# The stretch ahead of the loop of a fused attention and feed-forward kernel: who rounds and squares the second weight matrix, and in which order the queues are written

## The reference

```python
x = x + conv_ref(ln_over_channels(x))      # attention
t = tokens(x)                              # 16 x 192 tokens of 512 channels
t = t + ffn_ref(ln(t), w1, w2)

def conv_ref(x):
    avg, mx = mean(x over pixels), max(x over pixels)
    x = x * sigmoid(mlp(avg) + mlp(mx))            # fc1, relu, fc2
    s = concat(mean(x over channels), max(x over channels))
    return x * sigmoid(conv7x7(s))

def bitlinear(x, w):
    rms = rsqrt(max(mean(w * w), EPS))
    wq = clip(round(w * rms), -1, 1) / rms          # weights of -1, 0, 1
    scale = 127 / max(max|x| of each token, EPS)
    return (round(x * scale) / scale) @ wq.T

def ffn_ref(x, w1, w2):                             # 512 -> 2048 -> 512
    return bitlinear(gelu(bitlinear(x, w1)), w2)
```

## Time and profile before

| | us |
|---|---|
| median of 3 runs | 311.19 |
| lowest, highest | 310.03, 312.21 |
| the profiled execution | 311.29 |
| its span in the trace | 309.3 |
| TensorE busy | 265.9 |
| VectorE busy | 249.7 |
| ScalarE busy | 217.1 |
| GpSimd busy | 165.6 |

### The profile page before, as it was taken

How to read it: one execution, slowest core, us unless ns; L and a number is a source line. 1 busy time by engine, 2 the same in 40 slices (tenths; PEclk the granted TensorE clock), 3 DMA queues, 4 the chain that set the end, 5 groups by cost and what they waited for, 6 DMA issues and landing times.

```text
span 309.3 us, 5830 instructions
## 1 busy us (share of the span) xinstructions
PE 265.9 (86%) x1826; PEld 153.4 (50%) x1834; DVE 249.7 (81%) x556; ACT 217.1 (70%) x442; POOL 165.6 (54%) x267
## 2 busy tenths in 40 slices
PE   2457659696699999999999999999999987999974
PEld 2345634564356465645565555555555544444431
DVE  0673889989699989998998999899989997788410
ACT  1863687579476978687778876787678846676831
POOL 9506655416855385648555765566656563346410
PEclk9999965969999999999999999999999999899998
DMA  7999100002253129412931393439223713073693
GB/s 202 389 392 401 45 1 0 2 2 57 42 141 70 24 46 246 96 34 54 252 72 35 69 237 70 37 69 256 53 50 72 151 39 68 17 174 72 74 209 102
DMA packets 71077, 34.19 MB, mean 111 GB/s; under 512 B 52040, under 2 KB 68424, under 8 KB 70536
## 3 DMA queue, kind: packets, MB, share of 16 engines
q1 hardware_dynamic: 69300, 32.78, 43.1%
q10 hardware_dynamic: 1748, 1.05, 1.2%
HBM read 14.94 MB, written 6.29 MB: 69 GB/s over the span
## 4 chain that ended last, share of the span: by engine, by line
DVE 40%; PE 36%; issue 10%; ACT 4%; POOL 4%; ACTq 2%; DMA 1%; another core or an unknown queue 1%; SPq 1%; DVEq 0%; POOLq 0%
PE ps_o L1201 12%; DVE amax L883 8%; PE ps_h L1190 6%; PE ps_t L1190 6%; DVE t L856 6%; PE front L1120 3%; DVE st L858 3%; DVE amax L869 3%; DVE pv L824 3%; PE small L1166 2%; DVE cen L868 2%; DVE junk_v L909 2%; DVE st L782 2%; PE front L1210 2%; DVE res L900 2%
## 5 line engine op out<-in xcount | busy, mean ns | idle before, releaser
L1201 PE MATMUL ps_o<-w2T,hq 128*128 128x512 f16 x384 | 92.7, 379 | 1.1 <-DMA hq<-w_raw 1.1
L488 POOL TENSOR_SCALAR w_room<-w_room,q 128x1024 f32<-128x1024 f32 x48 | 57.1, 1201 | 51.4 <-DVE q L893 50.9
L883 DVE TENSOR_REDUCE amax<-w_room 128x1 f32<-128x1024 f32 (+1 forms) x48 | 57.2, 1208 | 2.3 <-ACT w_room L550 2.2
L1190 PE MATMUL ps_h<-w1T,xq 128*128 128x512 f16 x208 | 54.0, 403 | 1.1 <-ACT xq L550 0.7
L1201 PEld LDWEIGHTS ps_o<-w2T,hq 128*128 128x128 f16 x384 | 36.3, 98 | 36.0 <-DMA hq<-w_raw 2.1
L550 ACT ACTIVATE w_raw<-w_room 128x1024 f16<-128x1024 f16 x48 | 50.4, 1052 | 0.6 <-POOL w_room L488 0.6
L550 ACT ACTIVATE w_room<-ps_h,s 128x512 f32<-128x512 f32 x52 | 35.0, 688 | 13.1 <-PE ps_h L1190 12.0
L1190 PE MATMUL ps_t<-w1T,xq 128*128 128x512 f16 x176 | 42.0, 382 | 0.0
L550 ACT ACTIVATE w_room<-ps_t,s 128x512 f32<-128x512 f32 x44 | 30.2, 687 | 8.0 <-PE ps_t L1190 5.6
L1190 PEld LDWEIGHTS ps_h<-w1T,xq 128*128 128x128 f16 x208 | 20.1, 103 | 23.9 <-issue 3.9
L550 ACT ACTIVATE junk_m<-front 128x192 bf16<-128x192 f32 x64 | 20.6, 332 | 14.7 <-DVE pooled L795 14.7
(11 more groups left out here) (125 smaller groups left out, 450.5 us busy)
## 6 DMA issues: line engine op xcount, KB each, us to landing
out<-w_room SPq DMA_DIRECT2D x16, 384.0 KB, 3.0
x_in<-in_x SPq DMA_DIRECT2D x14, 384.0 KB, 5.1
w_room<-in_L_ffn_w SPq DMA_DIRECT2D x4, 1024.0 KB, 8.8
w_raw<-in_L_ffn_w SPq DMA_DIRECT2D x4, 1024.0 KB, 12.0
x_in<-in_x ACTq DMA_DIRECT2D x2, 384.0 KB, 3.8
hq<-w_raw SPq DMA_TRANSPOSE x48, 3.1
fc_raw<-in_L_conv_fc_w ACTq DMA_DIRECT2D x2, 128.0 KB, 4.2
taps_rev<-in_L_conv_sa_w SPq DMA_DIRECT2D x1, 0.2 KB
```

The lines of the kernel that those rows point to most:

```text
L488: pool.tensor_scalar(part, part, q2[tile.par][:, 0:1], MAGIC, ALU.mult, ALU.add).then_inc(g_rounded, 1)
L883: chain.mark(dve.tensor_reduce(amax2[:, i:i + 1], w1_room[:, first + i * F // 2:first + (i + 1) * F // 2 + i], AX.X, ALU.max, apply_absolu ...
L1190: last = pe.matmul(banks[b], xq[tile.pair.par][:, tile.s, k, :], w1T[:, k, b * 512:(b + 1) * 512], start=(k == 0), stop=(k == NC - 1))
L1201: last = pe.matmul(ps_o[:, :], hq[tile.par][:, k, :], w2T[:, k, :], start=(k == 0), stop=(k == NF - 1))
```

## The change

All edits are ahead of the loop. The loop's bodies are the same.

- SyncE issues five of the eight tap loads, ScalarE three.
- ScalarE squares three quarters of w2 instead of two, VectorE one instead of two. ScalarE does the first two earlier: one ahead of pair 0's channel gate, one ahead of pair 0's channel sums. The third comes behind the first gelu of tile 0.
- GpSimd rounds all of w2, in eight pieces, behind `round_x` of tile 1. VectorE rounds none.
- GpSimd normalises pair 1 in two steps around `round_x` of tile 0, and pair 2 in two steps around `round_g` of tile 1.
- On TensorE the convolution of pair 0 stands ahead of the second turn of w1 instead of the third; tile 0's four blocks alternate with pair 1's four turns; tile 1's blocks and pair 1's gates alternate with w2's eight turns; two of pair 2's three turns of x stand ahead of w2's last turns. ScalarE's and VectorE's lists follow that.

```diff
-        SQUARES_BY_VECTOR = [(3,), (2, 3)]
+        SQUARES_BY_VECTOR = [(3,), (3,)]
...
-            load_taps(sp, range(W // 2))
+            load_taps(sp, range(W - 3))
...
             def round_weights(k, raw):
                 pool.wait_ge(w_rms_ready, k + 1)
-                for i in range(4) if k == 0 else (1, 3):
+                for i in range(4):
                     part = quarter(k, raw, i)
-                    pieces = (part[:, 0:2, :], part[:, 2:4, :]) if k == 0 else (part,)
+                    pieces = (part[:, 0:2, :], part[:, 2:4, :]) if k == 0 else (part[:, 0:F // 2], part[:, F // 2:F])
...
             round_weights(0, w1_raw)
-            normalise1(Pair(1), 0, 1, 2)
             rstd2(Tile(Pair(0), 0))
+            normalise1(Pair(1), 0, 1)
             round_x(Tile(Pair(0), 0))
+            normalise1(Pair(1), 2)
             weight_rms(1)
-            round_weights(1, w2_raw)
             rstd2(Tile(Pair(0), 1))
             round_x(Tile(Pair(0), 1))
+            round_weights(1, w2_raw)
             round_g(Tile(Pair(0), 0))
             rstd2(Tile(Pair(0), 2))
             round_x(Tile(Pair(0), 2))
+            normalise1(Pair(2), 0, 1)
             round_g(Tile(Pair(0), 1))
-            normalise1(Pair(2), 0, 1, 2)
+            normalise1(Pair(2), 2)
...
-            load_taps(act, range(W // 2, W))
+            load_taps(act, range(W - 3, W))
...
             squares(0, w1_raw, w1_loaded, (2,))
+            squares(1, w2_raw, w2_loaded, (0,))
             gate_channels(pair0)
             copy_caT(pair0)
+            squares(1, w2_raw, w2_loaded, (1,))
             for s in range(NT):
                 sum_channels(Tile(pair0, s))
...
-            copy_weights(0, (0, 2))
+            copy_weights(0, (0,))
             gate_tokens(pair0)
-            copy_weights(0, (4, 5, 6, 7))
-            squares(1, w2_raw, w2_loaded, (0,))
+            copy_weights(0, (2, 4, 5, 6, 7))
...
             def weight_sum(k):
-                dve.wait_ge(squares_done, 3 + 2 * k)
+                dve.wait_ge(squares_done, 3 + 3 * k)
...
-            def round_weights(k, raw):
-
-                dve.wait_ge(w_rms_ready, k + 1)
-                for i in (0, 2):
-                    part = quarter(k, raw, i)
-                    dve.tensor_scalar(part, part, w_rms[:, k:k + 1], MAGIC, ALU.mult, ALU.add).then_inc(w_even_rounded, 1)
...
             def turn_weights(k, raw, banks):
                 for n in banks:
-                    i = n // 2
-                    if k == 0:
-                        pe.wait_ge(w_pool_rounded, n + 1)
-                    elif i % 2:
-                        pe.wait_ge(w_pool_rounded, 8 + i // 2 + 1)
-                    else:
-                        pe.wait_ge(w_even_rounded, i // 2 + 1)
+                    pe.wait_ge(w_pool_rounded, 8 * k + n + 1)
...
-            turn_weights(0, w1_raw, (0, 1))
+            turn_weights(0, w1_raw, (0,))
             pe.wait_ge(band_ready, 2)
             conv(pair0)
-            turn_weights(0, w1_raw, (2, 3, 4, 5, 6, 7))
+            turn_weights(0, w1_raw, range(1, 8))
```

More of the change, by code:

```diff
@@ L662, in _ @@
             act.wait_ge(masks_ready, 2)
[L663 removed]
+            copy_weights(0, (0,))
             gate_tokens(pair0)
[L665 to L666 removed]
+            copy_weights(0, (2, 4, 5, 6, 7))
             copy_xq(Tile(pair0, 0), 0)
+            gelu(Tile(pair0, 0), None, h_start, (0,))
+            squares(1, w2_raw, w2_loaded, (2,))
             token_mean(pair1, 0, 1)
[L669 to L673 removed]
+            gelu(Tile(pair0, 0), None, h_start, (1,))
+            token_mean(pair1, 1, 0)
+            gelu(Tile(pair0, 0), None, h_start, (2,))
+            token_mean(pair1, 2, 1)
+            gelu(Tile(pair0, 0), None, h_start, (3,))
+            token_mean(pair1, 3, 0)
+            copy_xq(Tile(pair0, 1), 1)
+            gelu(Tile(pair0, 1), None, h_start, (0,))
             copy_weights(1, (0,))
[L675 to L676 removed]
             gate_channels(pair1)
+            gelu(Tile(pair0, 1), None, h_start, (1,))
+            copy_caT(pair1)
+            copy_weights(1, (2,))
+            gelu(Tile(pair0, 1), None, h_start, (2,))
+            sum_channels(Tile(pair1, 0))
+            copy_weights(1, (3,))
+            sum_channels(Tile(pair1, 1))
+            gelu(Tile(pair0, 1), None, h_start, (3,))
+            sum_channels(Tile(pair1, 2))
             copy_weights(1, (4,))
[L679 to L680 removed]
+            copy_x(Tile(pair2, 0), 1)
+            copy_x(Tile(pair2, 1), 0)
             copy_weights(1, (6, 7))
[L682 to L687 removed]
             pack_g(Tile(pair0, 0), 0)
             pack_g(Tile(pair0, 0), 1)
[L690 to L692 removed]
+            copy_xq(Tile(pair0, 2), 1)
             copy_x(Tile(pair2, 2), 0)
@@ L901, in add_ffn, with squares @@
                                          t[tile.pair.par][:, tile.s, :], ALU.mult, ALU.add).then_inc(res_ready, 1)
-            def squares(k, raw, loaded):
-                for i in SQUARES_BY_VECTOR[k]:
+            def squares(k, raw, loaded, quarters):
+                for i in quarters:
                     dve.wait_ge(loaded[i], 16)
@@ L984, in _ @@
                 token_max(pair0, k, k % 2)
-            squares(0, w1_raw, w1_loaded)
+            squares(0, w1_raw, w1_loaded, (3,))
             hidden(pair0)
@@ L994, in _ @@
             weight_units(0)
+            channel_stats(pair1, 0, 1)
+            sum_conv(pair0)
             copy_weights(0, (1,))
-            stats1(pair1, 0, 1, 2)
-            sum_conv(pair0)
-            copy_weights(0, (3,))
             token_gate(pair0)
             add_attention(Tile(pair0, 0))
+            copy_weights(0, (3,))
+            channel_stats(pair1, 2)
+            aggregate(pair1, 0, 1, 2)
             centre(Tile(pair0, 0))
+            squares(1, w2_raw, w2_loaded, (3,))
+            weight_sum(1)
             token_max(pair1, 0, 1)
-            squares(1, w2_raw, w2_loaded)
-            weight_sum(1)
-            token_max(pair1, 1, 1)
             weight_floor(1)
-            token_max(pair1, 2, 0)
-            round_weights(1, w2_raw)
+            token_max(pair1, 1, 0)
+            token_max(pair1, 2, 1)
+            add_attention(Tile(pair0, 1))
+            token_max(pair1, 3, 0)
+            centre(Tile(pair0, 1))
             weight_units(1)
-            add_attention(Tile(pair0, 1))
             dve.wait_ge(w_turned, 8)
@@ L1306, in _ @@
+            b = turn_xq(Tile(pair0, 1), 1, b)
             fc1(pair1)
+            ffn_in(Tile(pair0, 1), h_start, (0,))
+            turn_weights(1, w2_raw, (0,))
+            fc2(pair1)
+            ffn_in(Tile(pair0, 1), h_start, (1,))
+            turn_weights(1, w2_raw, (1,))
+            turn_ca(pair1)
+            turn_weights(1, w2_raw, (2,))
+            ffn_in(Tile(pair0, 1), h_start, (2,))
+            a = spread_ca(Tile(pair1, 0), 0, a)
+            b = spread_ca(Tile(pair1, 1), 1, b)
@@ L1316, in _ @@
[L1316 to L1325 removed]
+            a = turn_x(Tile(pair2, 1), 0, a)
+            turn_weights(1, w2_raw, (6, 7))
@@ L1327, in body @@
+            conv(pair1)
+            b = turn_xq(Tile(pair0, 2), 1, b)
+            a = turn_x(Tile(pair2, 2), 0, a)
+            weights_ready(1)
             def body(pair, attend, normalise, turn):
```

76 lines of the change are left out of this document (22 added, 54 removed).

## The result

The changed kernel takes **319.82 us** (median; 319.18 to 320.01), the kernel before 311.28 beside it on the same chip (310.03 to 312.21). The ratio is **1.0278**, 95% interval 1.0247 to 1.031: the change makes the kernel 8.5 us slower by the medians. The forecast was 313.4, at most 317.2. That it would be slower was right; by how much was not.

What follows compares the result with a forecast made beforehand. The prediction took TensorE to bound the unedited loop, so only its start could move: parts summing to +1.6, plus 0.6 contention, put it 2.2 us later; added to the 311.19 median, 313.4 us (8 in 10: 308.8 to 317.2).

Steps and rivals of the forecast that it cites:

- The pause ahead of pair 2's first turn: TensorE's 2.36 us wait for pair 2's normalised x at the loop's start, said to almost vanish (-2.2).
- Rival (a): VectorE was the bound ahead of the loop and its relief counts: 308.0 us or less; chance 0.15.
- rival (d): The order of the edits is not taken as written; excluded by the prediction, no chance given.
- Rival (c): ScalarE's backlog with TensorE's low clock, tile 2's blocks taking 7.2 us instead of 3.6: 316.2 us; chance 0.20.
- 62.0 - 47.1 = 14.9: Stretch between the copies of tile 0 (forecast at 47.1) and tile 1 (62.0, a middle of 60.9 and 63.0).
- I counted 0.6 for each of two small subtractions in the gate: Contention allowance for VectorE's small gate instructions beside GpSimd; an exclusive lock would make the sum 1.0 larger.
- 0.6 for what contention with VectorE adds on GpSimd: Allowance added to the parts' sum of +1.6, as GpSimd's wide pieces took 3.0 instead of 2.2 beside VectorE.
- 1.8 for two tiles: Ahead of tile 0's copy: GpSimd's time to normalise two tiles of pair 1, 1.8 us.
- ScalarE loads the second table (1.28 us) and runs the first gelu at 49.7: Step behind tile 0's copy, forecast at 47.1; w2's third square then ends at 52.4.
- the forecast had charged 1.8: Two w2 squares moved forward on ScalarE: the last of pair 0's channel sums starts 1.8 us later, at 32.0.
- Rival (b): The edits balance: clock returns early, w2 lands as before, no contention; 310.9 us, chance 0.20.
- The largest term: ScalarE's backlog from tile 1's copy to the end of tile 2's: 19.3 us instead of 11.9 (+7.4).

Runs made afterwards that it cites:

- e7: The kernel before, with GpSimd rounding all of w2 in eight pieces at the old place and VectorE none; 0.9999 of the kernel before.
- e4: The changed kernel with a one-column gelu on ScalarE behind its last w1 copy, loading the second table early; 1.0255 of the kernel before.
- e1: The changed kernel with ScalarE's first two squares of w2 moved back behind its w1 copies; 1.0209 of the kernel before.
- e3: The changed kernel with GpSimd waiting for pair 0's channel gate ahead of rounding w1; 1.0271 of the kernel before.
- e2: The changed kernel with VectorE's square of w2 waiting for GpSimd's rounding of tile 0's input; 1.0195 of the kernel before.
- e9: e6 with GpSimd waiting for pair 1's channel gate ahead of its sixth piece of w2; 1.0103 of the kernel before.
- e12: e6 with GpSimd waiting for pair 1's gate ahead of its eighth piece, and two w2 pieces, two turns and a copy ahead of tile 1; 1.0037 of before.
- e6: The changed kernel with the edits of e1 and e2, and one table load by a gelu as ScalarE's first activation; 1.0067 of the kernel before.
- e5: The changed kernel with VectorE copying four of w2's eight turns instead of two, ScalarE the other four; 1.0345 of the kernel before.

## Why the prediction was wrong

**What was right.** The view that nothing in the loop moves: 226.3 us behind the first turn, 225.9 forecast. The table load at 6.06 (6.1), the wait for w2's load until 24.04 (23.7) and the tanh at 25.95 (25.9). The pause ahead of pair 2's first turn is gone, as said. Rival (a), that VectorE's relief counts, was given 0.15; at the old place in the queues e7 shows it worth nothing (0.9999), and rival (d) was excluded rightly. Rival (c) had its mechanism in part: the clock was at 0.50 in 64 to 68 and low again around tile 2's blocks, which took 5.0 us instead of 3.6 (86.62 to 91.61), 1.4 of the 1.8 that it named. The windows of the changed kernel:

```profile
84.00:88.00 4.00, 1.76 (x8) 0.72 (x7) 3.64 (x9) 2.96 (x5) 3.81 (x7) 0.75 0.44 86
88.00:92.00 4.00, 3.90 (x17) 1.52 (x16) 3.60 (x5) 2.42 (x4) 3.57 (x7) 0.82 0.24 46
```

The stretch from tile 0's copy to tile 1's, 14.64 us for 62.0 - 47.1 = 14.9, is right by luck: it holds 1.3 us of table load that the forecast had hidden, and without it e4 takes 13.35.

**Where the forecast lost its time.** The first turn was forecast at 85.6 and came at 91.71, 6.1 later. Of this 3.0 stand ahead of tile 0's copy (50.14 for 47.1), almost nothing between it and tile 1's, 2.3 between tile 1's and tile 2's, and 1.1 behind that, where TensorE's clock was low.

**The step that failed is the count of contention between VectorE and GpSimd,** "I counted 0.6 for each of two small subtractions in the gate" and "0.6 for what contention with VectorE adds on GpSimd". In the walk itself pair 0's gate got nothing: 25.9 to 28.2 is what it took before, 24.76 to 27.15. It was mis-sized at all three places:

- Pair 0's gate. Moving the tanh to 25.9 put the gate inside GpSimd's rounding. Three instructions took 2.4 us instead of 0.5. The copy of the gates ended at 29.9 (forecast 28.2), VectorE's second w1 copy at 42.6 (41.4). e1 and e3 each bring tile 0's copy 2.1 to 2.9 forward.
- VectorE's square of w2 beside GpSimd's normalising, ahead of tile 0: 3.54 us for "1.8 for two tiles". Both are in the list of edits, and the prediction never asked whether they run at once. e2 gives 2.1 us of tile 0's copy back, and 0.8% of the time.
- Pair 1's gate beside w2's pieces: 3.24 us instead of 0.5, and ScalarE waits 2.38 for it. What this was worth in the changed kernel no run shows; freed in e9 and e12, it was worth some 0.6 to 0.8, where the low clock kept TensorE busy meanwhile.

The Trainium skill ("SBUF — State Buffer", section "SBUF: two separate sides") names an exclusive lock, held for a whole instruction. By it a small subtraction waits up to one piece, and 1.05 and 1.06 us beside pieces of 1.10 agree with it. The square agrees too, as worked out from the rows: it ends at 45.26 + 2.69 = 47.95, which is 2.29 (its time alone) behind 45.66, when GpSimd's first tile of 45.05 was about done; GpSimd's second tile, 0.76 alone, then ends at 48.59, so it began only when the square was about over. The prediction cited the rule, gave 1.0 as what it would add, and took the smaller number.

**A second step was missing:** "ScalarE loads the second table (1.28 us) and runs the first gelu at 49.7". It took the load to be hidden behind the first product, as it was in the kernel before, where means and a square stood between and the load had no wait ahead of it (47.95). In the changed order the gelu follows tile 0's copy at once, and the load starts only when the gelu's wait ends. e4's trace measures 1.3 us.

**The sum.** e6 mends the first two of these meetings and the table load, and stands 0.67% over before, 2.1 us; the forecast said 2.2. That agreement is closer than the terms behind it. e6 also puts the two squares back, for whose own delay the forecast had charged 1.8, so by its terms e6 should stand 0.4 over before. The 1.7 between are not assigned to a cause; the second gate, which e6 leaves in place, is some 0.6 to 0.8 of it by the traces. What the forecast left out of the changed kernel is, for the larger part, the 6.6 us between e6 and it, less those 1.8. Rival (b), that the edits balance, rested on no contention and falls with it.

**The largest term was too small by 2.3 us, and for a reason only half right.** "Sum 11.9 + 4.6 + 0.8 + 2.0 = 19.3" gave tile 2's copy 18.7 us behind tile 1's; measured are 21.0. ScalarE's waits, put at 2.0, were 6.1, and its work was 14.9 instead of 16.7, partly because the 11.9 of before, "hardly idle", held 1.4 of waits (0.53, 0.27 and 0.60 in the trace of the kernel before). The backlog is real in the second half: from 76.43 on ScalarE has no wait. Ahead of that it waited for TensorE at the low clock and for pair 1's gate. And e5 shows that with two copies moved to VectorE tile 2 isn't sooner. In e6, TensorE is busy for all of 60 to 68 at a clock of 0.50, VectorE for 3.8 to 3.9 of every 4 us from 68 to 80, and ScalarE for all of 72 to 80. Three engines are close to their limit, and in e5 the relief of one moved the wait to the next. How much of the stretch each engine holds stays open.
